# Moving most of the K softmax's products, and the folding of the context, from the first stage into the first pass over the edges

## Chip, cores and metric

One Trainium2 chip, one of its cores. The metric is the device time of one execution in microseconds. Times are given as the median of several runs, and for one execution also as a profile, whose clock starts at the span's begin.

## The reference, cut to what matters

A graph of 6250 nodes with 256 features and 106250 edges (`src`, `dst`, sorted by `dst`, self-loops among them) goes through two layers. The parts that bear on the change are these, of the first layer:

```python
xn = layernorm(x)
# two graph convolutions, each: z = relu(segment_sum((h @ W)[src] * dinv[src] * dinv[dst], dst) + b); h = h + z
gnn = gcn_block(gcn_block(xn, W1, b1), W2, b2)
# linear attention with 4 heads of 32, the softmax of K over the nodes
q, k, v = split(xn @ W_qkv); k = softmax(k, over the nodes)
context = einsum('hld,hle->hde', k, v)
mix = einsum('hde,hld->hle', context, q * 32**-0.5) @ W_out + b_out
x = x + gnn + mix
```

A mixture-of-experts block and a second layer follow. Everything is fp32.

## The kernel before, in words

Nodes lie in T = 49 tiles of 128 (the last has 106). `XN` holds all tiles of the normalized rows, `ACC` (the first half of `AR`) the sums, and the other half of `AR` serves as `Kt` (the keys, 49 x 128 columns), then as `R` (the residuals, 49 x 256 columns). Behind `Kt`, from column `F0` on, lies room that `free` hands out. There are eight PSUM banks, `ps[0]` to `ps[7]`. Each `nc.Block()` is a stage: five engines run their own programs, meet at semaphores, and all wait for one another at its end.

**The first stage** (lines 298 to 721) normalizes the rows tile by tile, multiplies each by `[W1 | W_k]`, and leaves `h` in `ACC` and the keys in `Kt`. Meanwhile GpSimd and VectorE sort out the edges: 896 chunks of 128 edges, in an order by tiles, whose seven blocks of source and destination indices GpSimd fetches (L396). Then comes its end, in which these chains run side by side:
- VectorE finds the largest key, subtracts it from `Kt` in 13 groups `XC` of four tiles (L682, semaphore `s_sub`), and then goes through a loop over the seven lists: it casts a block of indices (L697, L698), scales two tiles of `ACC` by `dinv` (L701), and copies the previous list out of PSUM (`list_out`, L688, L689).
- ScalarE takes the exponential of each group (L429, `s_ex`) and scales, between these, the other tiles of `ACC` (`by_act`: five of seven, L437).
- TensorE, for each group, multiplies the exponentials of each tile with its rows (L508, into `ps[0]`) and with a column of ones (L510, into `ps[6]`), and from the sixth group on transposes a list (`visit_list`, L502). Then comes the folding: TensorE and VectorE in turn divide by the sum, multiply with `W_v`, keep the four diagonal blocks (`cT`), multiply with `W_out` and with `W_q` transposed (L517 to L527; L706 to L721). What results is `g0`, 256 x 256, by which the attention of a row is one product.
- SyncE's queue writes the 49 scaled tiles to `table[0]` in DRAM in order of tiles (L354), each as soon as it is scaled.

**The first pass** (lines 726 to 915) is the first graph convolution. GpSimd gathers, for each of 880 visits, the 128 rows of a chunk from `table[0]` into a ring of 16 buffers (L786). ScalarE makes the one-hot matrices of four visits at a time (L797, L801). TensorE multiplies one with the other (L837), two visits to a bank of `banks`, and VectorE adds the two products to `ACC` (L880). TensorE waits for the landing and for a free bank, VectorE for TensorE, and GpSimd for a free buffer (`s_mv`).

The function `turns` writes out the order by hand for each engine: turn i has 18 visits (`bound`), and ahead of its visits q = 0 to 17 stands `side(i, q)`, with two kinds of steps:
- for tile m = i (attention): ScalarE copies the normalized row (L812), TensorE transposes it (L847), ScalarE copies that (L816), TensorE multiplies with `g0` (L857), VectorE adds the bias to the residual (L906) and the product to it (L910), in `R`;
- for tile s = i - 1 (the convolution's second half): VectorE makes `b_z` and `b_x1` (L892, L898), TensorE transposes (L852), ScalarE copies (L820), TensorE multiplies with `W2` (L862), VectorE scales (L913) and SyncE's queue writes `table[1]` (L776). VectorE also writes `b_x1 + R` back to `XN` (L902).

The tile numbers come out of `slot`. Ahead of all this GpSimd clears the last tile of `R` (L781), and SyncE's queue loads `x` into `R` by four transfers of 12 tiles and a small one (L768, L770) and two rows of biases. A second pass like it follows.

Of the kernel before, what the change touches and what calls it, by code (L numbers as in the profile page):

```python
# [26 lines left out]
P = 128  # L27
# [78 lines left out]
def build(nc, A, out):  # L106

    with ExitStack() as ctx:
# [153 lines left out]
        kmax, nmat, cT = small[:, 640:768], small[:, 768:896], small[:, 896:1024]  # L262
# [3 lines left out]
        XC = [(q, min(q + 4, T)) for q in range(0, T, 4)]  # L266

# [30 lines left out]
        with nc.Block() as block:  # L298
# [10 lines left out]
            s_km, s_p, s_sub, s_ex, s_px, s_dv = (sem("c_" + n) for n in "km p sub ex px dinv".split())  # L309
# [91 lines left out]
            def _(a):  # L401
# [24 lines left out]
                scaled = 0  # L426
                for j, (t0, t1) in enumerate(XC):
                    a.wait_ge(s_sub, j + 1)
                    a.activation(Kt[:, t0:t1, :], Kt[:, t0:t1, :], ACT.Exp).then_inc(s_ex, 1)  # L429
                    if j == 0:  # L430
                        a.wait_ge(s_dv, 1)
                        a.wait_ge(s_hc, T)
                    upto = T * (j + 1) // len(XC)
                    for t in range(scaled, upto):
# [3 lines left out]
                    scaled = upto  # L438

            @block.tensor  # L440
            def _(pe):
# [55 lines left out]
                def visit_list(k):  # L497
# [3 lines left out]
                    for a in range(2):  # L501
                        pe.transpose(ps[(4, 2)[k % 2]][:, a * P:a * P + P], vst[:, (2 * (k % 2) + a) * P:(2 * (k % 2) + a + 1) * P],  # L502
                                     ident[:, :]).then_inc(s_vt, 1)
                for j, (t0, t1) in enumerate(XC):
                    pe.wait_ge(s_ex, j + 1)
                    for t in range(t0, t1):
                        n = LAST if t == T - 1 else P
                        pe.matmul(ps[0][:, 0:D], Kt[0:n, t, :], XN[0:n, t * D:(t + 1) * D], start=t == 0, stop=t == T - 1,  # L508
                                  skip_group_check=True)
                        ins = pe.matmul(ps[6][:, 0:1], Kt[0:n, t, :], one[0:n, :], start=t == 0, stop=t == T - 1, skip_group_check=True)  # L510
                    if j == len(XC) - 1:
                        ins.then_inc(s_px, 1)
                    if 5 <= j < 5 + VC:
                        visit_list(j - 5)
                pe.wait_ge(s_km, 3)
                for c in range(2):
                    ins = pe.transpose(ps[5][:, c * P:(c + 1) * P], pxn[:, c * P:(c + 1) * P], ident[:, :])  # L517
                ins.then_inc(s_p, 1)
                pe.wait_ge(s_km, 4)
                for c in range(2):  # L520
                    ins = pe.matmul(ps[7][:, 0:P], wv[:, c, :], pxT[:, c, :], start=c == 0, stop=c == 1)
                ins.then_inc(s_p, 1)
                pe.wait_ge(s_km, 5)
                pe.matmul(ps[5][:, 0:D], cT, wout, start=True, stop=True).then_inc(s_p, 1)
                pe.wait_ge(s_km, 6)
                for c in range(2):
                    ins = pe.matmul(ps[6][:, c * D:(c + 1) * D], wqT[:, c * P:(c + 1) * P], m1, start=True, stop=True)  # L527
                ins.then_inc(s_p, 1)

            @block.vector  # L530
            def _(v):
# [153 lines left out]
                def list_out(k):  # L685
                    v.wait_ge(s_vt, 2 * k + 2)
                    bank = ps[(4, 2)[k % 2]]
# [4 lines left out]
                for k in range(VC):  # L692
# [6 lines left out]
                    for t in left[2 * k:2 * k + 2]:  # L699
# [5 lines left out]
                v.wait_ge(s_px, 1)  # L705
                link(v.reciprocal(nmax, ps[6][:, 0:1]))  # L706
                link(v.tensor_scalar(pxn, ps[0][:, 0:D], nmax, 32.0 ** -0.5, ALU.mult, ALU.mult))
                v.sem_inc(s_km, 1)
                v.wait_ge(s_p, 4)
                link(v.tensor_copy(pxT.rearrange("p c n -> p (c n)"), ps[5][:, 0:D]))  # L710
                v.sem_inc(s_km, 1)
                v.wait_ge(s_p, 5)
                for q in range(4):
                    r = slice(32 * q, 32 * q + 32)
                    link(v.tensor_copy(cT[r, r], ps[7][r, r]))
                v.sem_inc(s_km, 1)
                v.wait_ge(s_p, 6)
                link(v.tensor_copy(m1, ps[5][:, 0:D]))
                v.sem_inc(s_km, 1)
                v.wait_ge(s_p, 7)  # L720
                link(v.tensor_copy(wreg[:, 1024:1536], ps[6][:, :]))  # L721
# [25 lines left out]
        Rt = R.rearrange("p (t d) -> p t d", d=D)  # L747
# [8 lines left out]
        s_x, s_tab, s_z = sem("b_x"), sem("b_tab"), sem("b_zero")  # L756
        banks = [0, 1, 2, 3, 5, 6]
# [4 lines left out]
        with nc.Block() as block:  # L762

            @block.sync
            def _(sp):
                sp.wait_ge(s_z, 1)
                for q in range(4):
                    sp.dma_start(Rt[:, 12 * q:12 * q + 12, :],  # L768
# [1444 lines left out]
```

## Time and profile before

| | |
|---|---|
| median of 3 runs | 4081.71 us (4075.95 to 4083.36) |
| the profiled execution | 4071.0 us |
| its span in the profile | 4069.3 us |
| mean granted TensorE clock | 0.895 of 2.4 GHz |
| first stage | 0 to 195 us |
| first pass, with its tail | 195 to 1317 us |

How to read it: an engine's busy time is the union of its instructions. Register and semaphore instructions and the issue of transfers are not counted as busy. A matmul of fp32 stands in the trace as two instructions, so one product of a tile is "x2", and a pair of visits "x4". "PEclk" is the granted clock as a share of 2.4 GHz, so 0.50 is 1.2 GHz. Idle time stands behind the bar with what ended it ("issue": nothing that the profile shows).

### The profile page before, as it was taken

What the parts mean: (1) busy time and instruction counts of PE and PEld (TensorE: products, weight loads), DVE (VectorE), ACT (ScalarE), POOL (GpSimd) and SP (SyncE); (2) the same over time, 40 slices, a digit from 0 to 9 for tenths busy, and PEclk for the clock granted to TensorE, in tenths of its full rate; (3) what the DMA queues carried; (4) which work ended last, traced back from release to release, by engine and by line L of the source; (5) the groups of instructions that cost most, each with busy time, mean ns of one, the idle gap of its engine ahead of it and who ended that gap; (6) DMA issues with size and microseconds to landing.
All of it is one profiled execution on the core that took longest, in us unless ns stands there. A gap on an engine that the chain in (4) does not pass through costs nothing. (4 is left out here: it accounts for less than half of the span.)

```text
span 4069.3 us, 58095 instructions
## 1 busy us (share of the span) xinstructions
PE 3277.6 (81%) x15028; PEld 2486.5 (61%) x15028; DVE 2367.5 (58%) x8479; ACT 1846.6 (45%) x4614; POOL 2698.7 (66%) x2858
## 2 busy tenths in 40 slices
PE   7767666766666787888888888776999999999998
PEld 4544444444444465666667666664777777777777
DVE  6444444444444455666666665363777777777776
ACT  4344444444443444544445442132555555555554
POOL 4177777777776777777777773043776676666762
PEclk9677877787877788999999998886999999999999
DMA  4353333333333434666666666642333333333331
GB/s 123 95 159 111 112 110 111 110 112 110 110 112 97 118 120 141 192 194 203 200 193 197 194 193 223 201 136 75 109 104 101 101 102 102 101 101 101 103 101 48
DMA packets 268651, 532.12 MB, mean 131 GB/s; under 512 B 57942, under 2 KB 165653, under 8 KB 268199
## 3 DMA queue, kind: packets, MB, share of 16 engines
q0 software_dynamic: 139296, 386.65, 32.2%
q1 hardware_dynamic: 129030, 141.78, 11.0%
q8 instruction: 126, 2.06, 0.2%
q14 instruction: 199, 1.62, 0.1%
HBM read 463.88 MB, written 64.34 MB: 130 GB/s over the span
## 5 line engine op out<-in xcount | busy, mean ns | idle before, releaser
L1847 POOL DMA_INDIRECT rows<-table,src_idx x880 | 845.0, 960 | 388.2 <-issue 219.9
L786 POOL DMA_INDIRECT rows<-table,src_idx x880 | 835.3, 949 | 268.1 <-issue 265.4
L1061 POOL DMA_INDIRECT rows<-table,src_idx x880 | 835.2, 949 | 267.9 <-issue 253.5
L880 DVE TENSOR_TENSOR AR<-AR,ps 128x256 f32 x880 | 370.6, 421 | 592.3 <-PE ps L837 529.1
L1224 DVE TENSOR_TENSOR AR<-AR,ps 128x256 f32 x880 | 370.1, 421 | 329.1 <-PE ps L1135 244.4
L1940 PE MATMUL ps<-rows,AR 128*128 128x256 f32 x1760 | 538.6, 392 | 7.9 <-issue 3.6
L2056 DVE TENSOR_TENSOR AR<-AR,ps 128x256 f32 x880 | 369.2, 420 | 177.2 <-PE ps L1940 101.6
L837 PE MATMUL ps<-rows,work 128*128 128x256 f32 x880 | 315.0, 486 | 172.9 <-DMA rows<-table,src_idx 151.7
L1135 PE MATMUL ps<-rows,work 128*128 128x256 f32 x1168 | 362.6, 419 | 74.4 <-DMA rows<-table,src_idx 64.9
L837 PEld LDWEIGHTS ps<-rows,work 128*128 128x128 f32 x880 | 188.0, 238 | 272.2 <-issue 141.9
L1940 PEld LDWEIGHTS ps<-rows,AR 128*128 128x128 f32 x1760 | 285.8, 193 | 72.0 <-issue 50.3
L1135 PEld LDWEIGHTS ps<-rows,work 128*128 128x128 f32 x1168 | 221.5, 208 | 151.6 <-issue 105.0
L797 ACT ACTIVATE work<-iota,dst_rel 128x128 f32<-128x128 f32 x440 | 140.5, 390 | 231.7 <-PE ps L837 231.4
L837 PE MATMUL ps<-rows,mring 128*128 128x256 f32 x440 | 163.8, 501 | 100.5 <-DMA rows<-table,src_idx 92.5
L1135 PE MATMUL ps<-rows,mring 128*128 128x256 f32 x592 | 186.7, 420 | 72.0 <-DMA rows<-table,src_idx 66.0
L1176 PE MATMUL ps<-wreg,work 128*128 128x512 f32 x392 | 209.3, 662 | 30.1 <-DVE work L1328 15.2
L1111 ACT ACTIVATE AR<-AR 128x1024 f32<-128x1024 f32 x49 | 51.8, 1057 | 393.9 <-DVE AR L1341 393.9
L837 PE MATMUL ps<-rows,gates 128*128 128x256 f32 x440 | 163.6, 500 | 83.1 <-DMA rows<-table,src_idx 67.7
L1092 ACT ACTIVATE work<-iota,dst_rel 128x128 f32<-128x128 f32 x584 | 185.8, 391 | 84.1 <-PE ps L1135 84.1
L1955 PE MATMUL ps<-AR 128*128 128x128 f32 x1176 | 176.0, 282 | 22.5 <-DVEq L2104 21.6
L837 PEld LDWEIGHTS ps<-rows,mring 128*128 128x128 f32 x440 | 97.3, 245 | 153.7 <-issue 79.6
L1955 PEld LDWEIGHTS ps<-AR 128*128 128x128 f32 x1176 | 159.9, 191 | 37.2 <-DVEq L2104 29.0
(508 smaller groups left out, 6687.0 us busy)
## 6 DMA issues: line engine op xcount, KB each, us to landing
AR<-in_L_ffn_Wd SPq DMA_DIRECT2D x48, 1024.0 KB, 7.2
rows<-table,src_idx POOLq DMA_INDIRECT x2640, 2.8
AR<-h_sorted SPq DMA_DIRECT2D x52, 512.0 KB, 3.9
table<-AR SPq DMA_DIRECT2D x147, 128.0 KB, 2.2
AR<-in_x SPq DMA_DIRECT2D x4, 1536.0 KB
out_x<-XN SPq DMA_DIRECT2D x48, 128.0 KB
AR<-in_L_ffn_bd SPq DMA_DIRECT2D x40, 128.0 KB, 8.3
y_sorted<-AR SPq DMA_DIRECT2D x40, 128.0 KB
```

Source lines behind the costliest of these rows:

```text
L786: g.indirect_dma_start(out=rows[:, u * D:(u + 1) * D], out_offset=None, in_=table[0], in_offset=bass.IndirectOffsetOnAxis(ap=src_idx[:, x: ...
L837: ins = pe.matmul(pair(x), hot[Q % 4][:, x % 4 * P:(x % 4 + 1) * P], rows[:, x % RING * D:(x % RING + 1) * D], start=True, stop=True)
L880: v.tensor_tensor(acc, acc, pair(y), ALU.add).then_inc(s_av, 1)
L1061: g.indirect_dma_start(out=rows[:, u * D:(u + 1) * D], out_offset=None, in_=table[1], in_offset=bass.IndirectOffsetOnAxis(ap=src_idx[:, x: ...
L1092: ins = a.activation(hot[Q % 3][:, k * P:(k + 1) * P], iota[:, :], ACT.Abs, scale=-1.0, bias=dst_rel[:, 4 * Q + k:4 * Q + k + 1])
L1135: ins = pe.matmul(pair(x), hot[Q % 3][:, x % 4 * P:(x % 4 + 1) * P], rows[:, x % RING * D:(x % RING + 1) * D], start=True, stop=True)
L1176: ins = pe.matmul(ps[3 + h][:, :], f_xT[:, c * P:(c + 1) * P], ff1[:, c, h * 512:(h + 1) * 512], start=c == 0, stop=c == 1)
L1224: v.tensor_tensor(acc, acc, pair(y), ALU.add).then_inc(s_av, 1)
L1847: g.indirect_dma_start(out=rows[:, u * D:(u + 1) * D], out_offset=None, in_=table[2], in_offset=bass.IndirectOffsetOnAxis(ap=src_idx[:, x: ...
L1940: ins = pe.matmul(ps[x // 2 % 2][:, x % 2 * D:(x % 2 + 1) * D], hot[Q % 4][:, x % 4 * P:(x % 4 + 1) * P], rows[:, u * D:(u + 1) * D], star ...
L1955: ins = pe.matmul(f_l1(k), w, f_xT[:, c * P:(c + 1) * P], start=c == 0, stop=c == 1)
L2056: v.tensor_tensor(acc, acc, ps[x // 2 % 2][:, y % 2 * D:(y % 2 + 1) * D], ALU.add).then_inc(s_av, 1)
```

## The change

Of the 13 groups of products only the first `XA` = 4 stay in the first stage, each between two visit lists (`context`, into `ps[4]` and `ps[6]`; the lists use `ps[0]` and `ps[2]`). The exponentials and products of groups 4 to 12 go into turns 0 to 8 of the pass, ahead of visits 1, 6 and 12; the folding goes into turns 9 and 10. Attention can begin only then: tile m = 0 and 1 in turn 11, two tiles in each turn to 20, from turn 21 on tile i - 1. As `Kt` and `XN` must live longer, there is no `R` any more: `x` comes tile by tile into three buffers `xr`, `b_x1 + x` goes to a ring of 16 tiles in the free room (`x1_of`), and the last addition of the attention writes `XN`. The memset of GpSimd goes. `banks` has five instead of six. In the first stage VectorE scales three tiles in each round of its loop instead of two, ScalarE four of seven instead of five.

```diff
+        XA = 4
         def by_act(t):
-            return t % 7 not in (2, 5)
+            return t % 7 not in (1, 3, 5)
+        def context(pe, t):
+            n = LAST if t == T - 1 else P
+            pe.matmul(ps[4][:, 0:D], Kt[0:n, t, :], XN[0:n, t * D:(t + 1) * D], start=t == 0, stop=t == T - 1, skip_group_check=True)
+            return pe.matmul(ps[6][:, 0:1], Kt[0:n, t, :], one[0:n, :], start=t == 0, stop=t == T - 1, skip_group_check=True)
 # first stage, ScalarE
-                for j, (t0, t1) in enumerate(XC):
...
+                a.wait_ge(s_dv, 1)
+                a.wait_ge(s_hc, T)
+                for j in range(XA + 1):
+                    for t in range(T * j // (XA + 1), T * (j + 1) // (XA + 1)):
+                        if by_act(t):
...
+                    if j < XA:
+                        t0, t1 = XC[j]
+                        a.wait_ge(s_sub, j + 1)
+                        a.activation(Kt[:, t0:t1, :], Kt[:, t0:t1, :], ACT.Exp).then_inc(s_ex, 1)
 # first stage, TensorE
-                for j, (t0, t1) in enumerate(XC):
...
+                pe.wait_ge(s_hc, T)
+                for k in range(VC):
+                    if 1 <= k <= XA:
+                        pe.wait_ge(s_ex, k)
+                        for t in range(*XC[k - 1]):
+                            context(pe, t)
+                    visit_list(k)
 # first stage, VectorE
-                    for t in left[2 * k:2 * k + 2]:
+                    for t in left[3 * k:3 * k + 3]:
 # pass
+        LAG = 11
+        MSLOTS = ((0, 2, 4, 6, 7, 8), (9, 11, 13, 15, 16, 17))
+        xr = [free(4096 + b * D, D) for b in range(3)]
+        FOLD_DVE = [(9, 1), (9, 6), (9, 11), (9, 16), (10, 4)]
+        FOLD_PE = [(9, 4), (9, 9), (9, 14), (10, 2)]
+        def x1_of(t):
+            return free(t % 16 * D, D)
+        def mixed(i):
+            if LAG <= i <= 2 * LAG - 2:
+                return [2 * (i - LAG), 2 * (i - LAG) + 1]
+            return [i - 1] if 2 * LAG - 1 <= i <= T else []
+        def mix_steps(i, q, k):
+            return [m for n, m in enumerate(mixed(i)) if MSLOTS[n][k] == q]
-        banks = [0, 1, 2, 3, 5, 6]
+        banks = [0, 1, 2, 3, 5]
 # pass, SyncE
                 for s in range(T):
+                    if s + 2 < T:
+                        if s > 0:
+                            sp.wait_ge(*bw.after(s - 1))
+                        x_tile(s + 2)
                     sp.wait_ge(*bh.after(s))
 # pass, GpSimd
-                g.memset(R[:, (T - 1) * D:T * D], 0.0).then_inc(s_z, 1)
 # pass, ScalarE
+                    if q == 1 and j < len(XC):
+                        a.activation(Kt[:, XC[j][0]:XC[j][1], :], Kt[:, XC[j][0]:XC[j][1], :], ACT.Exp).then_inc(s_ke, 1)
 # pass, TensorE (j = XA + i)
+                    if q in (6, 12) and j < len(XC):
+                        pe.wait_ge(s_ke, i + 1)
+                        t0, t1 = XC[j]
+                        for t in range(t0 if q == 6 else t0 + 2, min(t1, t0 + 2) if q == 6 else t1):
+                            ins = context(pe, t)
...
+                    if (i, q) in FOLD_PE:
+                        fold(FOLD_PE.index((i, q)))
-                    if q == 11 and has(m):
+                    for m in mix_steps(i, q, 3):
                         pe.wait_ge(*xt.after(m))
+                        pe.wait_ge(s_kv, 5)
 # pass, VectorE
+                    if (i, q) in FOLD_DVE:
+                        fold(FOLD_DVE.index((i, q)))
...
-                        v.wait_ge(s_x, 7 * 16)
+                        v.wait_ge(s_bias, 2 * 16)
...
-                        v.wait_ge(*r.after(s))
-                        v.tensor_tensor(XN[:, bass.ds(held["s"] * D, D)], b_x1, R[:, bass.ds(held["s"] * D, D)], ALU.add).then_inc(bw.sem, 1)
+                        v.wait_ge(s_x[s % 3], 16 * (s // 3 + 1))
+                        if s >= 16:
+                            v.wait_ge(*r.after(s - 16))
+                        v.tensor_tensor(x1_of(s), b_x1, xr[s % 3], ALU.add).then_inc(bw.sem, 1)
+                    for m in mix_steps(i, q, 4):
+                        v.wait_ge(*bw.after(m))
+                        v.tensor_tensor(x1_of(m), x1_of(m), b_row2, ALU.add).then_inc(rb.sem, 1)
+                    for m in mix_steps(i, q, 5):
+                        at = XN[:, bass.ds(tile_of(m) * D, D)]
+                        v.wait_ge(*gm.after(m))
+                        v.wait_ge(*rb.after(m))
+                        v.tensor_tensor(at, x1_of(m), ps[4][:, D:2 * D], ALU.add).then_inc(r.sem, 1)
```

The functions `fold` hold the former folding, statement by statement, with `ps[4]` and `ps[6]`.

## Rows read from the trace of the kernel before

**Rows 1.** The page, part 1: busy us (share of the span) and instructions

```profile
PE 3277.6 (81%) x15028; PEld 2486.5 (61%) x15028; DVE 2367.5 (58%) x8479; ACT 1846.6 (45%) x4614; POOL 2698.7 (66%) x2858
```

**Rows 2.** Windows: busy (instructions) of PE, PEld, DVE, ACT, POOL; granted clock; DMA share; GB/s

```profile
118.00:134.00 16.00, 4.81 (x15) 2.44 (x15) 13.04 (x62) 2.55 (x7) 6.00 (x6) 0.66 0.23 12
...
155.00:165.00 10.00, 10.00 (x34) 8.65 (x33) 0.00 (x0) 0.00 (x0) 0.00 (x0) 0.50 0.01 2
...
400.00:700.00 300.00, 203.74 (x636) 136.57 (x636) 130.75 (x317) 131.48 (x338) 227.14 (x240) 0.80 0.38 111
```

**Rows 3.** Costliest groups of the first pass: busy, mean ns | idle before, releasers

```profile
L786 POOL DMA_INDIRECT rows<-table,src_idx x880 | 835.3, 949 | 268.1 <-issue 265.4 <-PE ps L837 2.7
L880 DVE TENSOR_TENSOR AR<-AR,ps 128x256 f32 x880 | 370.6, 421 | 592.3 <-PE ps L837 529.1 <-DVE AR L880 5.1 <-issue 0.5
```

**Rows 4.** The gather's line: duration ns min/median/max, and its landing

```profile
L786 POOL DMA_INDIRECT rows<-table,src_idx x880: 942/946/1191, 195.7 to 1297.8; - x176
...
DMA to landing us min/median/max: 2.7/2.8/6.8
```

**Rows 5.** Timeline, TensorE, end of the first stage: start, us, engine, line, op, names, count

```profile
135.10 1.20 PE L508 MATMUL ps<-XN,AR 128*128 128x256 f32 x2
...
136.38 1.20 PE L508 MATMUL ps<-XN,AR 128*128 128x256 f32 x2
...
164.54 0.67 PE L502 MATMUL ps<-ident,rows 128*128 128x128 f32 x2
...
169.98 0.67 PE L502 MATMUL ps<-ident,rows 128*128 128x128 f32 x2
...
175.42 0.68 PE L508 MATMUL ps<-XN,AR 128*128 128x256 f32 x2
```

**Rows 6.** Timeline, VectorE, same stretch

```profile
140.50 0.23 DVE L697 CAST rows<-rows 128x128 f32<-128x128 int32 x1
...
140.84 0.67 DVE L701 TENSOR_SCALAR AR<-AR,dinv 128x256 f32<-128x256 f32 x2
...
165.25 0.29 DVE L688 CAST src_idx<-ps 128x128 int32<-128x128 f32 x1 [22.89 <-PE ps L502]
...
192.89 0.69 DVE L721 COPY wreg<-ps 128x512 f32<-128x512 f32 x1 [2.22 <-PE ps L527]
```

**Rows 7.** Timeline, ScalarE, same stretch

```profile
136.17 0.62 ACT L429 ACTIVATE AR<-AR 128x512 f32<-128x512 f32 x1
136.69 1.29 ACT L437 ACTIVATE AR<-AR,dinv 128x256 f32<-128x256 f32 x3
```

**Rows 8.** Timeline, SyncE's queue, the last of the 49 writes of the table

```profile
177.57 6.86 SPq L354 DMA_DIRECT2D table<-AR  x14
```

**Rows 9.** Timeline, GpSimd, the border between the two stages

```profile
195.02 0.31 POOL L781 MEMSET AR<- 128x256 f32 x1 [51.12 <-POOLq L123]
195.69 0.95 POOL L786 DMA_INDIRECT rows<-table,src_idx  x1 [0.36 <-issue]
```

**Rows 10.** Timeline, TensorE in the pass: one pair of visits at either clock

```profile
247.61 1.10 PE L837 MATMUL ps<-rows,gates 128*128 128x256 f32 x4 [1.44 <-DVE AR L880]
...
250.18 2.05 PE L837 MATMUL ps<-rows,work 128*128 128x256 f32 x4 [1.25 <-DMA rows<-table,src_idx]
```

**Rows 11.** Timeline, all engines, the end of the pass

```profile
1301.36 14.19 SPq L776 DMA_DIRECT2D table<-AR  x3
...
1306.79 1.91 PE L857 MATMUL ps<-wreg,work 128*128 128x256 f32 x4
...
1312.64 0.37 ACT L820 COPY work<-ps 128x256 f32<-128x256 f32 x1 [5.22 <-PE ps L853]
...
1313.06 1.13 PE L862 MATMUL ps<-wreg,work 128*128 128x256 f32 x4 [0.46 <-ACT work L820]
1314.23 0.49 DVE L913 TENSOR_SCALAR AR<-ps,dinv 128x256 f32 x1 [1.55 <-PE ps L862]
...
1317.35 0.20 POOL L1044 MEMSET wreg<- 128x128 f32 x1 [18.58 <-POOLq L762]
```

More of the change, by code:

```diff
@@ L501, in visit_list @@
                     for a in range(2):
-                        pe.transpose(ps[(4, 2)[k % 2]][:, a * P:a * P + P], vst[:, (2 * (k % 2) + a) * P:(2 * (k % 2) + a + 1) * P],
+                        pe.transpose(ps[(0, 2)[k % 2]][:, a * P:a * P + P], vst[:, (2 * (k % 2) + a) * P:(2 * (k % 2) + a + 1) * P],
                                      ident[:, :]).then_inc(s_vt, 1)
-                for j, (t0, t1) in enumerate(XC):
[L505 to L528, printed above, removed]
+                pe.wait_ge(s_hc, T)
[5 more added lines that the diff above has]
+                    visit_list(k)
             @block.vector
@@ L704, in _ @@
                 list_out(VC - 1)
[L705 to L721, printed above, removed]
         retire_sems()
@@ L755, in build @@
             Step(sem("b_" + n), 1) for n in "row tp xt gm rb r z x1 w btp bxt mm h".split())
-        s_x, s_tab, s_z = sem("b_x"), sem("b_tab"), sem("b_zero")
-        banks = [0, 1, 2, 3, 5, 6]
+        s_bias, s_tab = sem("b_bias"), sem("b_tab")
+        s_x = [sem(f"b_xin{b}") for b in range(3)]
+        s_ke, s_kp, s_kv, s_kl = (sem("b_k" + n) for n in "e p v l".split())
+        banks = [0, 1, 2, 3, 5]
         def pair(x):
@@ L807, in side @@
                 def side(i, q):
-                    m, s = i, i - 1
-                    if q == 0 and has(m):
+                    s, j = i - 1, XA + i
+                    if q == 1 and j < len(XC):
+                        a.activation(Kt[:, XC[j][0]:XC[j][1], :], Kt[:, XC[j][0]:XC[j][1], :], ACT.Exp).then_inc(s_ke, 1)
+                    for m in mix_steps(i, q, 0):
                         t = loads(mybir.EngineType.Activation, slot[0:1, m:m + 1], T - 1)[0]
@@ L812, in side @@
                         a.copy(r_row, XN[:, bass.ds(t * D, D)]).then_inc(row.sem, 1)
-                    if q == 7 and has(m):
+                    for m in mix_steps(i, q, 2):
                         a.wait_ge(*tp.after(m))
@@ L840, in visit, with fold @@
                         ins.then_inc(s_mv, 1)
-                def side(i, q):
-                    m, s = i, i - 1
-                    if q == 3 and has(m):
+                def fold(n):
+                    if n == 0:
+                        pe.wait_ge(s_kv, 1)
+                        for c in range(2):
+                            ins = pe.transpose(ps[4][:, c * P:(c + 1) * P], pxn[:, c * P:(c + 1) * P], ident[:, :])
+                    if n == 1:
+                        pe.wait_ge(s_kv, 2)
+                        for c in range(2):
+                            ins = pe.matmul(ps[6][:, 0:P], wv[:, c, :], pxT[:, c, :], start=c == 0, stop=c == 1)
+                    if n == 2:
+                        pe.wait_ge(s_kv, 3)
+                        ins = pe.matmul(ps[4][:, 0:D], cT, wout, start=True, stop=True)
+                    if n == 3:
+                        pe.wait_ge(s_kv, 4)
+                        for c in range(2):
+                            ins = pe.matmul(ps[6][:, c * D:(c + 1) * D], wqT[:, c * P:(c + 1) * P], m1, start=True, stop=True)
+                    ins.then_inc(s_kp, 1)
+                def side(i, q):
+                    s, j = i - 1, XA + i
+                    if q in (6, 12) and j < len(XC):
[3 more added lines that the diff above has]
+                            ins = context(pe, t)
+                            if t == T - 1:
+                                ins.then_inc(s_kp, 1)
+                    if (i, q) in FOLD_PE:
+                        fold(FOLD_PE.index((i, q)))
+                    for m in mix_steps(i, q, 1):
                         pe.wait_ge(*row.after(m))
```

58 lines of the change are left out of this document (31 added, 27 removed).

## The prediction

> **What bounds the kernel now.** I read the page first, then windows over the first 1320 us, then the groups, and last the timeline of each engine around the two borders of the stage that the change touches. The page's totals [rows 1] name no single bound: TensorE is at 81%, GpSimd at 66%, and stages with different limits are mixed in them. Only two stages are touched, so the question is what ends each of these.
>
> The first stage (layer norm, the K softmax, the tables) ends on TensorE. From 133.8 us it works through 49 products of the exponentials with the normalized rows. The reader is to see in [rows 5] that one tile takes 136.38 - 135.10 = 1.28 us, and that the granted clock in this stretch is 0.50 (1.2 GHz) with TensorE busy for 10.00 of 10 us and all others at zero [rows 2]. The seven visit lists are stuck in that chain: two of their transposes stand 169.98 - 164.54 = 5.44 us apart [rows 5], with four tiles between them, and VectorE sat idle for 22.89 us before it could read the first [rows 6]. After the products comes the folding of the context, back and forth between TensorE and VectorE; its last copy begins at 192.89 and takes 0.69, so it ends at 193.58 [rows 6]. ScalarE's scaling and the writes of the table had ended long before: the last 14 writes ran from 177.57 to 184.43 [rows 8]. GpSimd's first gather starts at 195.69 [rows 9].
>
> The first pass is bound by GpSimd, and by nothing else. 880 gathers take 835.3 us, and the 268.1 us idle before them are 265.4 of "issue" [rows 3]; (835.3 + 268.1) / 880 = 1.254 us each. The 2.7 us put down to TensorE are nine waits of 0.3, no longer than an issue gap. The gather's duration hardly varies, 942 to 1191 ns with a median of 946 [rows 4]. VectorE waits for TensorE for 529.1 us in the pass [rows 3]: in the window from 400 to 700 TensorE is busy 68%, VectorE and ScalarE 44% each, at a mean clock of 0.80 [rows 2]. A turn has 18 visits, or 22.6 us. So work added to the pass costs nothing while TensorE does not fall so far behind that the ring of 16 buffers fills, and work taken out of it gains nothing.
>
> **What leaves the first stage.** 33 of the 49 products (33 x 1.28 = 42.2 us) and the whole folding (about 8 us) go. The stage doesn't get shorter by the sum of these, because other chains come up behind. I walk them.
>
> VectorE: its loop over the seven lists begins at 140.50, after the 13 subtractions, which stay. Casts take 140.84 - 140.50 = 0.34 us; a scaling is 0.67 / 2 = 0.33 [rows 6], now three in each turn of the loop (21 instead of 14), so 1.0. TensorE: the first list's transposes now wait for those casts (about 141.0), and the products come behind them. Four products and a list take 5.44 us at clock 0.50, as before, so the fifth list's transposes start at 141.0 + 4 x 5.44 = 162.8. VectorE reads a list 165.25 - 164.54 = 0.71 us after its transposes start [rows 5, 6]; that is 163.5, and some 0.4 us for the two copies. Only then comes the seventh round: casts, and the scalings of tiles 43, 45 and 47, done at 164.6, 164.9 and 165.2. ScalarE: 28 scalings at 1.29 / 3 = 0.43 us and four exponentials of 0.62 [rows 7] from 133.1 us, five of the scalings already before that: 23 x 0.43 + 4 x 0.62 = 12.4, done near 145.5, off the path. The queue of SyncE: a write takes 6.86 / 14 = 0.49 us [rows 8]. It writes in order of tiles, so tile 43 waits for its scaling and tile 48 is issued about 164.7 + 5 x 0.49 = 167.2. At the end of the pass the last of three writes ends its issue at 1301.36 + 14.19 = 1315.55, which at 0.49 each began about 1315.1, and the next stage's first instruction is at 1317.35 [rows 11], some 2.2 us after it. The next stage thus begins at 169.4, and with no memset ahead of the first gather (0.67 us today, [rows 9]) I put the gather at 169.5. **The gain is 195.69 - 169.5 = 26.2 us.**
>
> Its upper bound is a full clock in this stretch, at which a product takes half as long (two matmuls in 0.68 instead of 1.20, [rows 5]). Then SyncE's queue sets the end: tile 1 is scaled at about 141.2, 48 more writes x 0.49 = 23.5, last issue 164.7, gather at 167.0, gain 28.7. I take the low clock, since 36 us of unbroken work were done at 0.50 in the same place, and the new stretch is only 24 us long.
>
> The Trainium skill (TensorE: Matmul & The Clock Gate, Part 1) says that sustained activity releases the throttle to the full 2.4 GHz. The trace speaks against it here: busy for all of 155 to 165 us, and the clock is 0.50. By the rule the gain would be 28.7, by the row it is 26.2.
>
> **What enters the pass.** TensorE gets four products in each of turns 0 to 7 and one in turn 8: 4 x 1.28 = 5.1 us at the low clock. Turns 0 to 10 lose one attention step each, turns 11 to 20 have two. An attention step is two transposes and four matmuls, 1.91 us for the four at the low clock [rows 11] and about 0.84 for the transposes (as 0.67 for the two of a list, [rows 5], and some wait): 2.75. At the full clock it is some 1.6 (1.13 for the four, [rows 11]). A pair of visits takes 2.05 us at the low clock, 1.10 at the full one [rows 10]. So a turn in which the clock never rises costs 9 x 2.05 + 2 x 2.75 = 23.9 us today, 9 x 2.05 + 2.75 + 5.1 = 26.3 in turns 0 to 7, and 9 x 2.05 + 3 x 2.75 = 26.7 in turns 11 to 20; at the full clock 14.1 and 14.7. GpSimd needs 22.6. The clock's mean of 0.80 lets TensorE hold that with room, and the ring holds 14 visits, less 2.8 us of landing [rows 4]: 14 x 1.254 - 2.8 = 14.8 us of lag before GpSimd feels it. I take nothing. VectorE's additions (folding some 4 us once, one step of 0.4 us twice in turns 11 to 20) and ScalarE's nine exponentials (0.6 each) lie in engines at 44%. The banks go from six to five: TensorE may be 10 visits ahead instead of 12, and it is 2 or 3 ahead, as it runs right behind the landing. The pair at 247.61 is put down to VectorE [rows 10], but twelve visits earlier had long been added then. Nothing.
>
> **SP's queue in the pass.** Five large loads become 49 of 128 KB, issued one or two turns ahead; a turn leaves that queue empty most of the time. The four long loads delayed the first gathers (up to 6.8 us to landing, [rows 4]), which the ring hid; losing them gains nothing. What 49 more issues do to the gathers has no row. All lengthening of gathers today is 835.3 - 880 x 0.946 = 2.8 us; the bounds are 0 and another 2.8. I take 0.
>
> **The tail of the pass.** The last turn now has the attention of tile 48 besides its own step. Its transposes fit in while VectorE works, but its four matmuls stand between the transposes of the step and its product. These are ready when ScalarE's copy (1312.64 + 0.37) is done [rows 11]; the inserted group needs 0.9 at the full clock and 1.9 at the low one from about 1312.6. So +0.4 to +1.9, and I take +0.7, since the clock was high there.
>
> **Sum.** -26.2 + 0.7 = -25.5 us. The profiled execution took 4071.0 us for a span of 4069.3; after, 4045.5. It lies 10.7 us below the median of the runs (4081.7, from 4076.0 to 4083.4), so the median goes to 4056.2. Later stages run the same instructions and only start earlier.
>
> **Rivals.**
> - *The clock rises in the first stage's products* (above): 4081.7 - 28.7 + 0.7 = 4053.7. Chance 0.07.
> - *TensorE becomes the pass's bound* (the slower side). Place: turns 0 to 8 and 11 to 20. If the clock stays at 0.50 there, it loses 26.3 - 22.6 = 3.7 us in each of nine turns and 4.1 in each of ten, 74 in all, less the ring's 14.8: +59, and 4115. The clock was low for 36 us on end with the same products, which speaks for it; 300 us at a mean of 0.80 and GpSimd without one real wait speak against. It decides when the lost time passes 25.5 + 14.8 = 40 us, which is all of turns 0 to 8 and two more. Chance 0.04. Low in turns 0 to 8 alone gives 33 - 15 = 18 us of stall and 4074, no measurable change: 0.04.
> - *The first stage ends later than I walked it*, since a list, the index rows or the write queue is late by some 5 to 11 us: 4061 to 4067. For it: the VectorE loop is now in lock step with three others. Chance 0.07.
> - *My forecast*, between 4081.7 - 28.4 and 4081.7 - 21.5: 0.78.
>
> **How the numbers follow.** The forecast's own bounds are 4053 and 4060; three runs spread by 7 us, so I widen by some 5 on the low side and take in the late first stage above: 4048 to 4067. A measurement of this kernel can tell 0.2%, or 8 us. Faster: 0.78 + 0.07 + 0.07 = 0.92; same 0.04; slower 0.04.
>
> **What would show it.** The first gather near 169.5 with 880 of them ending 1103 us later; a granted clock of 0.50 from 141 to 165; list transposes 5.44 us apart; the last write of the table issued near 167. Waits of the gathers for TensorE above 3 us would prove the lag; gathers with a mean above 952 ns the cost of the added transfers; a gap of more than 20.3 us from the start of the last gather to the next stage a worse tail (today it is 1317.35 - 1297.8 = 19.55, [rows 4, 11]).

## The result, and the profile after

| | before | after |
|---|---|---|
| median of the first four runs each | 4078.8 us (4070.0 to 4083.4) | 4039.2 us (4035.5 to 4043.0) |
| the profiled execution | 4071.0 us, span 4069.3 | 4041.0 us, span 4039.3 |
| first gather of the pass | 195.7 us | 167.9 us |
| start of the next stage | 1317.4 us | 1289.4 us |

The ratio is 0.9906, with a 95% interval from 0.9885 to 0.9926: the change makes the kernel faster. I had said 4056.2, from 4048 to 4067. The direction was right and the measured median lies outside the range, 8.8 us below its low end.

The page of the changed kernel, part 1:

```profile
PE 3250.8 (80%) x15028; PEld 2481.6 (61%) x15028; DVE 2368.7 (59%) x8486; ACT 1842.5 (46%) x4607; POOL 2700.9 (67%) x2857
```

The totals hardly differ from [rows 1]: TensorE has as many matmuls as before and is busy for 27 us less, GpSimd for 2 us more.

The groups of the first pass (busy, mean ns, idle before and its releasers), to be set beside [rows 3]:

```profile
L782 POOL DMA_INDIRECT rows<-table,src_idx x880 | 835.8, 950 | 292.4 <-issue 262.6 <-POOLq L123 24.6 <-PE ps L835 5.2
L906 DVE TENSOR_TENSOR AR<-AR,ps 128x256 f32 x880 | 370.4, 421 | 602.0 <-PE ps L835 533.2 <-DVE AR L906 8.5 <-issue 2.0
```

The gather is as it was: 835.8 us for 880, 262.6 of issue, and TensorE's 5.2 us are again waits of 0.3 (4.6 us of them stand in a second profile of either kernel). The 24.6 us are the border ahead of the first gather.

The end of the first stage, engine by engine, TensorE first (answers to [rows 5]):

```profile
140.46 0.66 PE L507 MATMUL ps<-ident,rows 128*128 128x128 f32 x2 [9.03 <-DVE rows L685]
...
145.89 0.67 PE L507 MATMUL ps<-ident,rows 128*128 128x128 f32 x2
...
150.00 0.42 PE L507 MATMUL ps<-ident,rows 128*128 128x128 f32 x2
...
152.79 0.42 PE L507 MATMUL ps<-ident,rows 128*128 128x128 f32 x2
...
156.91 0.44 PE L507 MATMUL ps<-ident,rows 128*128 128x128 f32 x2 [0.69 <-DVE rows L685]
```

VectorE ([rows 6]), then SyncE's queue ([rows 8]) and GpSimd ([rows 9]):

```profile
146.60 0.29 DVE L675 CAST src_idx<-ps 128x128 int32<-128x128 f32 x1 [2.61 <-PE ps L507]
...
156.77 0.87 DVE L688 TENSOR_SCALAR AR<-AR,dinv 128x256 f32<-128x256 f32 x3
...
158.15 0.28 DVE L676 COPY dst_rel<-ps 128x128 f32<-128x128 f32 x1
```

```profile
136.50 0.24 SPq L355 DMA_DIRECT2D acc_at<-at_dram  x1
136.78 0.35 SPq L361 DMA_DIRECT2D table<-AR  x1
...
140.60 23.50 SPq L361 DMA_DIRECT2D table<-AR  x48
```

```profile
142.34 0.94 POOL L403 DMA_INDIRECT rows<-dst_pad,newton  x1 [0.30 <-issue]
167.90 0.94 POOL L782 DMA_INDIRECT rows<-table,src_idx  x1 [24.62 <-POOLq L123]
```

Windows (busy and instructions of PE, PEld, DVE, ACT, POOL; granted clock; DMA; GB/s), answering to [rows 2]:

```profile
140.00:148.00 8.00, 7.54 (x25) 6.64 (x26) 5.39 (x24) 3.89 (x10) 2.67 (x3) 0.50 0.77 251
150.00:156.00 6.00, 6.00 (x43) 5.56 (x41) 3.21 (x14) 0.00 (x0) 0.00 (x0) 1.00 0.81 267
400.00:700.00 300.00, 208.96 (x693) 146.27 (x694) 137.24 (x336) 137.82 (x358) 227.41 (x239) 0.82 0.41 117
```

The reader is to see three things. The list transposes are 5.43 us apart at first (140.46 to 145.89) and 2.79 later (150.00 to 152.79): the clock rose from 0.50 to 1.00 between 148 and 150. VectorE's last scaling ended at 157.64. And SyncE's queue, which issued tile 0 at 136.78, has to wait for tile 1, the first that VectorE scales, until 140.60; from there it issues the other 48 writes in 23.50 us, 0.49 each, to 164.10. So it is the write queue that ends the stage, and the first gather follows 3.8 us after it.

The last turn of the pass, [rows 11] before:

```profile
1283.01 0.48 DVE L939 SCALAR_TENSOR_TENSOR gates<-AR,dinv,bias_rows 128x256 f32<-128x256 f32 x1
...
1284.38 1.03 PE L883 MATMUL ps<-wreg,work 128*128 128x256 f32 x4
...
1285.25 1.03 PE L888 MATMUL ps<-wreg,work 128*128 128x256 f32 x4
...
1286.31 0.48 DVE L962 TENSOR_SCALAR AR<-ps,dinv 128x256 f32 x1 [0.34 <-PE ps L888]
...
1289.43 0.20 POOL L1093 MEMSET wreg<- 128x128 f32 x1 [17.99 <-POOLq L751]
```

Here the clock was high; the four matmuls of the attention (L883) stand ahead of the product (L888), but from `b_z` (1283.01) to the end of the last scaling (1286.79) are 3.78 us, against 3.66 before.

### The profile page after: what moved, and what is told of

Read it like the earlier page. It is cut to its first block and busy times, and to the rows that moved or that the text cites. A ratio compares the mean times of both kernels' runs of the same rounds, so it can differ in the third digit from the quotient of the medians.

```text
span 4039.3 us, 58284 instructions
## 1 busy us (share of the span) xinstructions
PE 3250.8 (80%) x15028; PEld 2481.6 (61%) x15028; DVE 2368.7 (59%) x8486; ACT 1842.5 (46%) x4607; POOL 2700.9 (67%) x2857
## 5 line engine op out<-in xcount | busy, mean ns | idle before, releaser
L782 POOL DMA_INDIRECT rows<-table,src_idx x880 | 835.8, 950 | 292.4 <-issue 262.6
L1184 PEld LDWEIGHTS ps<-rows,work 128*128 128x128 f32 x1168 | 224.9, 211 | 157.5 <-issue 94.3
L835 PE MATMUL ps<-rows,gates 128*128 128x256 f32 x440 | 150.3, 464 | 93.4 <-DMA rows<-table,src_idx 75.0
L1141 ACT ACTIVATE work<-iota,dst_rel 128x128 f32<-128x128 f32 x584 | 185.8, 391 | 68.1 <-PE ps L1184 67.9
L1207 PE MATMUL ps<-AR 128*128 128x256 f32 x640 | 175.1, 402 | 10.5 <-DMA AR<-in_L_ffn_bd 10.5
```

Source lines behind the costliest of these rows:

```text
L782: g.indirect_dma_start(out=rows[:, u * D:(u + 1) * D], out_offset=None, in_=table[0], in_offset=bass.IndirectOffsetOnAxis(ap=src_idx[:, x: ...
L835: ins = pe.matmul(pair(x), hot[Q % 4][:, x % 4 * P:(x % 4 + 1) * P], rows[:, x % RING * D:(x % RING + 1) * D], start=True, stop=True)
L1141: ins = a.activation(hot[Q % 3][:, k * P:(k + 1) * P], iota[:, :], ACT.Abs, scale=-1.0, bias=dst_rel[:, 4 * Q + k:4 * Q + k + 1])
L1184: ins = pe.matmul(pair(x), hot[Q % 3][:, x % 4 * P:(x % 4 + 1) * P], rows[:, x % RING * D:(x % RING + 1) * D], start=True, stop=True)
```

## The experiments

Theory: the gain is what the first stage loses, until the write queue comes up behind; the pass takes all that is added for nothing; the rest of the difference in medians (39.6 us) is scatter. Rivals: a saving outside the two stages; TensorE ends the first stage or bounds the pass.

### 1. Is it 28 or 40 us? Both kernels again

No edit. The changed kernel:

> The changed kernel once more, unaltered, beside the kernel before on one chip. The two profiles at hand put 27.9 us of the gain into the first stage (the first gather at 167.9 instead of 195.7) and the next stage starts 28.0 us earlier; the spans differ by 30.0 us, the medians of the runs by 39.6. Theory 'scatter': the change is worth 28 to 31 us, and the rest is how the earlier runs fell; the ratio comes out at 0.9925 to 0.9933. Rival 'a further saving outside the two stages': the ratio stays at 0.9905 (some 39 us), and a second profile shows a later stage shorter by some 10 us.

The kernel before:

> The kernel before, unaltered, against itself. Theory 'scatter': ratio 1.000 within 0.002, and a second profile whose stage borders (1317.4, 2651.6, 2767.3, 2811.2 in the first) move by 1 to 5 us each in the stages that are bound by TensorE, while the first gather stays at 195.7 within 0.3 and the 880 gathers of the first pass take 1102 to 1103 us. Rival: the profile repeats to within 1 us at the span's end, so that execution is reproducible and the 10 us must be a real difference.

Measured: the changed kernel 4040.8 us, ratio 0.9924 (0.9911 to 0.9937). The kernel before against itself: 0.9993 (0.9982 to 1.0005), its twelve runs from 4054.8 to 4077.7. The 28 runs of it on this chip, one of 10386 us left out, have a mean of 4071.1 and a standard deviation of 5.6; five of the changed kernel have a mean of 4041.8. That is 29.3 us. First gather at 168.7 against 196.9, next stage at 1290.7 against 1317.9.

What follows: the four first runs of the kernel before, with a mean of 4077.7, lay high (the three that I had before the prediction have 4080.3); the profiled execution's 4071.0 was the usual value. Why those runs lay high is not shown. The ratio of 0.9924 falls between the two expected ones, next to that of 'scatter'. The expectation that a repeated profile of the kernel before would move by up to 5 us was too wide: the borders of the later stages moved by 0.5 to 0.9 us, and its first gather by 1.2 instead of 0.3. The two spans, 4069.3 and 4069.7, are as close as the rival asked for; but the twelve runs beside them spread over 23 us, so that this closeness is luck and doesn't make the 10 us a real difference.

### 2. The pass: each product twice

```diff
+                            context(pe, t)
                             ins = context(pe, t)
```

> The changed kernel, with each product of groups 4 to 12 in the pass made twice (so these tiles count double in the softmax's sums). Adds 33 products to turns 0 to 8: 5.1 us per turn at the low clock, 2.6 at the full one. Theory 'GpSimd alone bounds the pass': from the first to the last gather 1102.6 us as before, the gathers wait for TensorE for less than 8 us in total (5.2 in the changed kernel, in waits of 0.3), first gather to next stage 1121.5 within 0.7. Rival 'TensorE is near the bound in turns 0 to 8': with a turn at the low clock of 9 x 2.05 + 2.75 + 10.2 = 31.4 us against 22.6, the ring of 16 runs full and the pass grows by 10 to 60 us.

Measured: 4041.1 us, first gather 168.2, last 1270.9, so 1102.7 us. Waits of GpSimd (in total, times, longest), and TensorE's groups from 168 to 371 us:

```profile
POOL rows L782 <- issue: 262.0, 860, 0.3
...
POOL rows L782 <- PE ps L835: 5.8, 19, 0.3
```

```profile
L283 PE MATMUL ps<-XN,AR 128*128 128x256 f32 (+1 forms) x132 | 46.6, 445 | 0.0
...
L284 PE MATMUL ps<-one,AR 128*128 128x1 f32 (+1 forms) x132 | 19.4, 217 | 0.0
```

Twice as many matmuls of the products (132 instead of 66 in either group) stand there, and GpSimd doesn't notice: 5.8 us in nineteen waits of 0.3. In this kernel the doubled tiles count twice in the context. From the first gather to the next stage it took 1123.9 us, against 1121.5 and 1122.0 in the two profiles of the changed kernel. The difference lies wholly behind the last gather (21.2 us against 18.9 and 18.6), where the last turn ran largely at the low clock (5.54 us from `b_z` to the end of the last scaling, against 3.78); experiment 6 comes back to this.

### 3. The first stage: the write queue in the order of scaling

```diff
+                acts = [[t for t in range(cut[j], cut[j + 1]) if by_act(t)] for j in range(XA + 1)]
+                dves = [t for t in range(T) if not by_act(t)]
+                order = sum(acts[:-1], []) + dves[0:3] + acts[-1] + dves[3:]
-                for t in range(T):
+                for n, t in enumerate(order):
```

The load of `acc_at` moves behind the first 22 writes, so this run changes two things at once.

> The changed kernel, with SyncE's queue in the first stage writing the tiles of the table in the order in which they are scaled (ScalarE's first four groups, then VectorE's first three, and so on), and the load of acc_at behind the first 22 writes. Theory 'the write queue ends the first stage': in the changed kernel it issues 29 writes back to back from 149.9 to 164.1 while VectorE is done at 158.2; with the new order it has 22 of the 49 out by 142 and ends right behind VectorE's last scaling (157.6), last issue at 158 to 159, first gather at 160 to 161.5, 6.5 to 8 us earlier than 167.9, and the kernel 6.5 to 8 us faster. Rival 'TensorE's products end it': nothing moves, first gather at 167.5 to 168.

Measured: 4039.0 us, ratio 0.9913 (0.9898 to 0.9927); by the means of five runs, 4037.5 against 4041.8, 4.3 us below the changed kernel. By the medians it is 1.8, and the intervals of the two ratios overlap; the traces tell more than the times here. SyncE's queue and GpSimd:

```profile
128.42 14.90 SPq L366 DMA_DIRECT2D table<-AR  x22
143.36 0.29 SPq L361 DMA_DIRECT2D acc_at<-at_dram  x1
143.69 15.79 SPq L366 DMA_DIRECT2D table<-AR  x27
```

```profile
163.30 0.94 POOL L787 DMA_INDIRECT rows<-table,src_idx  x1 [19.44 <-POOLq L123]
```

The first gather came at 163.3, 4.6 us before 167.9 and 5.4 before 168.7, and the next stage began at 1283.9 instead of 1289.4 and 1290.7; this confirms that the queue ended the stage. It is less than the 6.5 to 8 expected: the last issue ended at 159.48, right behind VectorE (158.68) as expected, but from the last issue's start to the first gather it takes 4.3 us and not the 2.3 that I had assumed.

The row of 22 writes hides a wait: five are issued from 128.42 to 130.72 and the next only at 134.14, as ScalarE takes the first exponentials (132.5) before it scales more tiles. The gain comes from these early issues. In the changed kernel the queue stood behind the load of `acc_at` until 136.50 and then behind tile 1 until 140.60, and waited for no tile after that. The order of the tiles and the place of the load weren't tried one by one. In the new kernel the queue waits for VectorE's scalings again near the end (until 155.40 and 158.19), so it isn't the bound any more.

### 4. The first stage: six groups instead of four

```diff
-        XA = 4
+        XA = 6
```

> The changed kernel with six groups of products in the first stage instead of four (XA = 6; turns 0 to 6 take the rest). Theory 'the write queue ends the first stage, TensorE has slack in it': VectorE's last scaling needs only the fifth list's read-out, which stays, so it moves by at most 1 us; the last list's read-out moves from 158 to about 163 and still ends before the last write's landing; first gather at 167.9 to 169.0 as in the changed kernel (167.9 and 168.7). Rival 'TensorE's products end the stage': first gather 5 to 10 us later, at 173 to 179.

This run and those below were on two other chips, on which 56 to 75 of the 880 gathers wait for something that the profile puts down to a DMA, and the kernel before takes 4627.9 and 4675.5 us; `at_dram` is issued some 23 us later there. Times are compared only on one chip. SyncE's queue, VectorE and GpSimd of this kernel:

```profile
159.84 28.92 SPq L361 DMA_DIRECT2D table<-AR  x49
```

```profile
179.96 0.87 DVE L688 TENSOR_SCALAR AR<-AR,dinv 128x256 f32<-128x256 f32 x3
...
185.01 0.28 DVE L676 COPY dst_rel<-ps 128x128 f32<-128x128 f32 x1
```

```profile
192.58 0.95 POOL L782 DMA_INDIRECT rows<-table,src_idx  x1 [26.01 <-POOLq L123]
```

The writes end at 188.76, VectorE's last scaling at 180.83 and its last list at 185.29, both before them: with eight more products TensorE still isn't last. From the issue of `at_dram` to the first gather it takes 43.4 us, against 41.9 in the changed kernel on the first chip and 42.4 in a later profile on a slow one. So it costs 1.0 to 1.5 us, and the rival's 5 to 10 us are not there. This compares single profiles, of different chips.

### 5. Why the clock rose earlier than in the kernel before

Two edits of the kernel before. Without the one-column products, except for two tiles:

```diff
+                        if t in (0, T - 1):
-                        ins = pe.matmul(ps[6][:, 0:1], Kt[0:n, t, :], one[0:n, :], start=t == 0, stop=t == T - 1, skip_group_check=True)
+                            ins = pe.matmul(ps[6][:, 0:1], Kt[0:n, t, :], one[0:n, :], start=t == 0, stop=t == T - 1, skip_group_check=True)
```

> The kernel before without the products with the column of ones, except for the first and the last tile (the sums of the keys' exponentials are left out for the others). Asks why TensorE's clock stays at 0.50 from 134 to 170.5 in the kernel before, busy all the time, while it rises 8 to 12 us after the first product in the changed one. Theory 'the one-column products hold it down': the clock is at 1.00 by 145 to 150, and the products end 15 to 20 us earlier. Rival 'it rises once the transposes of the lists stand in the chain': no rise before the first list's transposes (now at about 159, as a tile takes some 1.0 instead of 1.28 us).

The lists behind groups 2 to 8:

```diff
-                    if 5 <= j < 5 + VC:
-                        visit_list(j - 5)
+                    if 2 <= j < 2 + VC:
+                        visit_list(j - 2)
```

> The kernel before with the seven lists' transposes behind groups 2 to 8 of the products instead of 5 to 11; nothing is left out. Theory 'the clock rises once the transposes stand in the chain': first list at about 149, the clock at 1.00 by 155 to 162 instead of 170.5, and the stage ends 5 to 8 us earlier (first gather at 187 to 191 instead of 195.7 and 196.9). Rival 'it rises some 36 us after TensorE has become busy, whatever it does': the rise stays at 169 to 172 and the first gather at 195 to 197.

Windows of TensorE (busy, clock, DMA share, GB/s), without the one-column products and then with the early lists:

```profile
156.00:159.00 3.00, 3.00 (x9) 0.50 0.44 99
159.00:162.00 3.00, 3.00 (x14) 0.90 0.53 163
162.00:165.00 3.00, 3.00 (x15) 1.00 0.84 260
```

```profile
159.00:162.00 3.00, 3.00 (x10) 0.50 0.65 190
180.00:183.00 3.00, 3.00 (x11) 0.50 0.53 173
183.00:186.00 3.00, 3.00 (x19) 0.92 0.56 187
```

Without the one-column products TensorE starts on the products at 153.58, and the clock is at 0.90 in the window from 159 to 162, some 6 us later and before the first list's transposes (167.20). With them and with the lists early it starts at 155.97, and the clock stays at 0.50 to 183.5: 27.5 us, 12 after the first list (171.35). A third profile of the kernel before, on the third chip (experiment 6), stayed low for longest, from its first product at 156.76 to 206:

```profile
203.00:206.00 3.00, 3.00 (x12) 0.50 0.39 130
206.00:209.00 3.00, 3.00 (x20) 0.98 0.68 225
```

So in all four profiles with a one-column product behind each of the 49 tiles the clock stayed low for 27 to 49 us, and in the one without them for 6. That is what the first theory expected, on one profile; its rival, that the lists bring the rise, fell with it. The second run's rival, a rise some 36 us after TensorE has become busy, fell too: it was 27.5 us there, and 37, 35 and 49 in the three profiles of the kernel before. Its theory is open: 12 us after the first list lies within the 6 to 13 expected, but the kernel before has 6, 4 and 19, so the lists bring no fixed delay either. In the changed kernel, with a list ahead of the first product, it took 7 to 12 us. What decides when the clock rises stays open. The first gathers (190.0 and 212.6) can't be compared with the expected ones, as these two ran on a chip without a profile of the kernel before.

### 6. No products in the first stage at all

```diff
-        XA = 4
+        XA = 0
-        LAG = 11
+        LAG = 15
-        FOLD_DVE = [(9, 1), (9, 6), (9, 11), (9, 16), (10, 4)]
+        FOLD_DVE = [(13, 1), (13, 6), (13, 11), (13, 16), (14, 4)]
```

`FOLD_PE` moves likewise, and the writes go in the order of scaling.

> The changed kernel with none of the products left in the first stage (XA = 0, so turns 0 to 12 take them, the folding is in turns 13 and 14 and attention starts in turn 15), and SyncE's queue writing ScalarE's 28 tiles first, then VectorE's 21. Theory 'the first stage ends on whatever chain comes up behind, and the pass takes any of it for nothing': 28 writes from 128 to 142, the last of the 49 issued at 152 to 154, first gather at 156 to 158.5 (the write-order kernel had 163.3), 880 gathers in 1102 to 1103 us as ever, so 4.5 to 7 us below the write-order kernel and 9 to 11.5 below the changed one. Rival 'with 49 products TensorE becomes the pass's bound': the gathers wait for TensorE for more than 8 us and the first gather's gain is lost by the next stage's start.

Measured on the second chip (the kernel before: 4627.9): 4607.2 us, ratio 0.9953 (0.9939 to 0.9967); first gather at 183.4. The single run of the kernel with six groups on that chip took 4606.5 with its first gather at 192.6. So the 9 us were not in the time there; 5.8 of them went behind the last gather (25.3 us to the next stage against 19.5). That was inconclusive, so the three kernels ran beside each other:

> The changed kernel, unaltered, beside the two that follow on one chip, since the kernel without products in the first stage ran on a chip on which every gather is slower (before: 4627.9 us). Theory 'the gain is what the first stage loses': first gather 26 to 29 us earlier than in the kernel before on this chip, the pass from first gather to next stage the same within 2 us, ratio 0.992 to 0.9945. Rival 'a saving outside these two stages': 35 us or more.

> The kernel with the writes of the table in the order of scaling, once more: 3.5 to 5.5 us below the changed kernel by the first gather (it was 163.3 against 167.9 and 168.7) and by the median; ratio to the kernel before 0.991 to 0.9925.

> No products in the first stage, writes in the order of scaling, once more beside the others. Theory 'the write queue ends the stage': the first gather comes 1 to 4 us before that of the write-order kernel, as the queue issues 49 writes without a wait (28 of them at 0.66 us each on the other chip), not 4.5 to 7. If the pass takes the 49 products for nothing, the median falls by as much, 6 to 9 us below the changed kernel; if TensorE near its bound in turns 0 to 12 and 15 to 28 gives some back, it lies within 3 us of the write-order kernel.

> The kernel before, for its profile on the same chip: first gather to next stage's start, and the borders of the later stages, to be set beside those of the three above. Theory 'scatter': later stages differ by 1 to 4 us in either direction.

| third chip | median us | ratio (interval) | first gather | next stage |
|---|---|---|---|---|
| before | 4675.5 | | 224.9 | 1513.0 |
| changed | 4649.3 | 0.9945 (0.9932 to 0.9959) | 191.8 | 1485.0 |
| writes in order | 4644.5 | 0.9926 (0.9913 to 0.9939) | 185.8 | 1478.7 |
| no products, writes in order | 4641.7 | 0.9927 (0.9912 to 0.9941) | 185.3 | 1475.0 |

The write order is worth 6.0 us at the first gather and 4.9 in the median, a little more than expected in the one and as expected in the other. Leaving out the products as well gives 0.5 us at the first gather, less than the 1 to 4 expected: the queue issues 28 writes in 19.1 us at that time, 0.68 each, and stays the bound. Its median is 2.7 us lower, inside the scatter of five runs, and 7.6 below the changed kernel: both expected outcomes, 6 to 9 below the one and within 3 of the other, were met, so the time doesn't tell them apart. The trace does: from the first gather to the next stage the pass takes 1289.7 us with all 49 products in it, and 1292.9 with 33 of them (one profile each), so it gives nothing back. The write order had the lowest first gather and the earliest next stage of the versions with products in the first stage, on both chips on which it ran.

On this chip the first stage loses 33.1 us, more than the 26 to 29 expected, and the next stage starts only 28.0 us earlier, so that the pass is 5.1 us longer, outside the 2 us expected. The first number is mostly the kernel before: there the clock stayed at 0.50 to 206 (experiment 5), and from its first product to its first gather it took 68.1 us, against 61.9 on the first chip. Waits of GpSimd in the changed kernel's pass:

```profile
POOL rows L782 <- issue: 233.8, 765, 0.8
POOL rows L782 <- DMA dst_pad<-rows: 171.6, 74, 3.8
...
POOL rows L782 <- PE ps L835: 24.1, 40, 3.3
```

Here GpSimd waits 171.6 us for what the profile calls a DMA, which on the first chip it didn't at all; the kernel before waits 167.8 for it and 19.9 for TensorE. The transfer named, `dst_pad`, belongs to the first stage, so what these gathers really waited for isn't shown. The 880 gathers take 1266.2 us, and 1265.6 in the kernel before. The 5.1 us are thus in the tail: from the last gather to the next stage the changed kernel takes 27.0 us, the kernel before 22.5. Part of it is the last turn at the low clock:

```profile
1477.14 0.48 DVE L939 SCALAR_TENSOR_TENSOR gates<-AR,dinv,bias_rows 128x256 f32<-128x256 f32 x1
...
1478.71 1.91 PE L883 MATMUL ps<-wreg,work 128*128 128x256 f32 x4
...
1480.42 1.43 PE L888 MATMUL ps<-wreg,work 128*128 128x256 f32 x4
...
1481.89 0.48 DVE L962 TENSOR_SCALAR AR<-ps,dinv 128x256 f32 x1 [0.70 <-PE ps L888]
```

From `b_z` to the end of the last scaling it takes 1482.37 - 1477.14 = 5.23 us, against 3.65 in the kernel before on this chip (1506.68 to 1510.33) and 3.78 in the changed one at the high clock. The other 2.9 us of the 4.5 lie ahead of `b_z`, which starts 19.1 us after the last gather and 16.2 in the kernel before; why isn't shown.

## Why the prediction was right or wrong

- **The bound of the pass: right.** 880 gathers took 1102.1 and 1102.6 us before, 1102.6 and 1103.4 after, and 1102.7 with twice the moved products. Expected was nothing from the work put in, and 0.5 to 0.8 us came. My sign for a lag, more than 3 us of waits for TensorE, was set too low: it was 5.2 and 4.6 us, but a second profile of the kernel before has 4.6 as well.
- **The first stage: right that the other chains come up behind TensorE's, wrong in which of them ends it, and 1.6 to 2 us short.** I said 26.2 us by the first gather; it was 27.8 in the first pair of profiles and 28.2 in the second. The forecast took the clock at 0.50 to the end of the products, which put the last write's issue at 167.2. It rose at 148.6 (and at 153.5 in the second profile), so the queue became the bound, as in the rival with chance 0.07: that one had tile 1 at 141.2 and 48 more writes of 0.49, the trace has 140.60 and 141.35 and 48 writes in 23.5 us. The last write was issued at 163.6 instead of 167.2. By luck the error was halved by a second one: behind the last issue I counted 2.2 us to the next stage, taken from the end of the pass, and 0.1 to the gather, and it takes 4.3 at this border. The difference isn't in moving the bytes: the traffic of the writes has ended by 165.5, and the next stage's first instruction is at 167.26, at least 1.8 us later; at the end of the pass it is at most 0.9 (1288.5 to 1289.4). The stage's end also clears its semaphores, which the end of the pass doesn't. That this makes the difference was argued from the code alone.
- **The row against the rule.** The Trainium skill (TensorE: Matmul & The Clock Gate, Part 1) says that sustained activity gives the full clock; the row of before had some 36 us without it, and I took the row. The trace bears out neither alone: TensorE was busy without a gap for 35 to 49 us at 0.50 in the kernel before, and the full clock came after 7 to 12 us in the changed one. I had concluded from 36 us without a rise that 24 us would have none either; but the mix of matmuls in the new stretch was another. Experiment 5 has the numbers.
- **The tail: +0.7 forecast, -0.6 to +0.2 measured on the first chip** (18.9 and 18.6 us from the last gather to the border, against 19.55 and 18.4), +1.6 in the last turn on the third chip, where the clock was low. The bounds of +0.4 to +1.9 were the right ones for the low clock; at the high one the added matmuls cost 0.1.
- **What failed is the anchor, the last step of the sum.** The sum gave -25.5 us, and 4071.0 - 25.5 = 4045.5 for the profiled execution; that took 4041.0. I then moved the forecast up by 10.7 us, to the median of three runs, and so to 4056.2. Repeated, the kernel before has a mean of 4071.1: the profiled execution was typical, and the three runs were not. That step is 10.6 us of the 17.0 by which I missed; 1.8 are the first stage and 0.3 the pass (a tail 0.9 us shorter than forecast, gathers 0.6 longer), and the last 4.3 are the later stages and the scatter of four runs, which can't be told apart. From 4071.1 the same sum gives 4045.6, against the 4041.8 of the repeated runs. The scatter of a single run (standard deviation 5.6) was put at "some 5" for the range of a median, but it was added on one side of a wrong centre.
- **Later stages.** From the start of the second pass to the span's end the changed kernel was 2.1 us shorter than before in the first pair of profiles, 4.9 shorter in the second, and 0.8 longer on the third chip. No effect of the change can be told there. The 10 us of the rival 'a further saving outside the two stages' aren't there.
- **The slower rival** (TensorE bounds the pass) did not come about. On the third chip GpSimd waits for TensorE for 24.1 us in the changed kernel, up to 3.3 at once, and 19.9 in the one before; on the first it is 5.2 and 4.6 against 2.7 and 4.6.

## What to carry to other kernels

When a chain is taken off the end of a stage, walk every other chain to its end, the queue that writes results above all: here its second write waited for a tile that another engine scaled late, behind a small load, and letting the ready tiles go first gave 4 to 6 us more. A stage bound by one engine's issue of gathers took a neighbour's work for less than 1 us of 1100, as long as a ring keeps the lag; doubling the work is a cheap way to ask how much room is left. Anchor an absolute forecast to as many runs as there are, the profiled one among them, and give the range their scatter.

## What the runs showed of the hardware that I had not expected

- TensorE, busy without a gap, stayed at 1.2 GHz for 35, 37 and 49 us in three profiles of a chain of 256-column products each followed by a one-column one; in the one profile without the one-column products the full clock came after some 6 us (a mean of 0.90 in the window from 159 to 162, where the first product was at 153.58).
- The write of a 128 x 256 tile costs SyncE's queue 0.49 us where it waits for nothing (48 in 23.50 us). On the two slow chips the first 28 writes of the kernel without products took 0.66 and 0.68 each, with ScalarE ahead of them, while GpSimd fetched index rows; that this was the reason isn't shown.
- Chips differ: the same kernel took 4071, 4628 and 4675 us. On the two slow ones GpSimd sat idle for 134 to 176 us in the first pass in waits that the profile puts down to a DMA, at the same duration of the gather instruction itself (median 946 to 949 ns).
